# Seven of 21 down products per chunk in three rounded passes instead of one fp32 product

## The reference

```python
scores = sigmoid(x @ gate_weight.T)            # 32 experts, 4 groups, top 2 groups, top 6 experts
g, u = x @ w_gate[e], x @ w_up[e]              # 128 -> 64 for every expert e
eo = (silu(g) * u) @ w_down[e]                 # 64 -> 128
routed = sum_e cw[:, e] * eo[e]
shared = (silu(x @ shared_w_gate) * (x @ shared_w_up)) @ shared_w_down
anchor = one of 16 small experts (128 -> 32 -> 128), by the best expert
out = routed + shared + 0.1 * anchor
```

## Time and profile before

| | |
|---|---|
| median of 3 runs (range) | 1450.74 us (1450.39 to 1451.39) |
| profiled execution, its span | 1452.6 us, 1450.8 us |
| TensorE busy | 1412.9 us (97%) |
| VectorE busy | 1111.2 us (77%) |
| ScalarE busy | 800.2 us (55%) |
| GpSimd busy | 287.6 us (20%) |
| mean granted TensorE clock | 0.995 of full speed |

### The profile page before, as it was taken

The page is one execution under the profiler, slowest core; times in us unless marked ns, Lnnn a source line. Parts: engine busy times, 40 slices in busy tenths (PEclk is TensorE's granted clock), DMA queues, the critical chain, the costliest instruction groups (busy, mean ns, idle before and its releaser), DMA issues.

```text
span 1450.8 us, 27512 instructions
## 1 busy us (share of the span) xinstructions
PE 1412.9 (97%) x9680; PEld 967.3 (67%) x9680; DVE 1111.2 (77%) x2521; ACT 800.2 (55%) x1909; POOL 287.6 (20%) x586
## 2 busy tenths in 40 slices
PE   5999999999989999999999999999899999999998
PEld 4666666666657667676766676676566666666665
DVE  8888888887677777777777777778767877787775
ACT  4344344433457777777777877777544233423422
POOL 1000000000124434444443444344400000000000
PEclk9999999999999999999999999999999999999999
DMA  6432323332300000000000000000033333333332
GB/s 231 162 132 105 112 97 124 107 117 97 116 30 2 2 2 2 2 2 1 2 2 2 2 2 2 1 2 2 2 120 104 126 109 121 110 119 116 119 112 87
DMA packets 59025, 98.07 MB, mean 68 GB/s; under 512 B 6160, under 2 KB 15504, under 8 KB 58896
## 3 DMA queue, kind: packets, MB, share of 16 engines
q1 hardware_dynamic: 58896, 96.38, 19.6%
HBM read 92.68 MB, written 3.67 MB: 66 GB/s over the span
## 4 chain that ended last, share of the span: by engine, by line
PE 86%; DVE 8%; ACT 3%; issue 2%; POOL 0%; DMA 0%; SPq 0%; POOLq 0%; DVEq 0%; ACTq 0%
PE banks L424 19%; PE banks L199 14%; PE banks L201 13%; PE banks L200 13%; PE banks L560 10%; PE banks L525 7%; PE banks L546 5%; PE banks L383 2%; PE banks L535 2%; DVE nmax L1297 2%; ACT work L859 1%; PE banks L395 1%; DVE q_lo L1286 1%; DVE ctx_lo L1317 1%; DVE stage L1312 1%
## 5 line engine op out<-in xcount | busy, mean ns | idle before, releaser
L803 ACT ACTIVATE work<-banks 128x512 f32<-128x512 f32 x320 | 190.9, 597 | 444.5 <-PE banks L201 435.2
L424 PE MATMUL banks<-work,wd 128*128 128x512 f32 x672 | 342.8, 593 | 0.6 <-DVE work L1179 0.4
L1205 DVE TENSOR_TENSOR work<-banks,work 128x512 f32<-128x512 f32 x320 | 220.7, 690 | 147.8 <-ACT work L803 143.4
L859 ACT ACTIVATE work<-banks,nmax 128x512 f32<-128x512 f32 (+3 forms) x512 | 264.4, 528 | 51.9 <-DVE nmax L1297 47.7
L1454 POOL TENSOR_SCALAR work<-work,rrec 128x512 f32<-128x512 f32 (+3 forms) x512 | 261.7, 533 | 0.0
L199 PE MATMUL banks<-xT_hi,wg_hi 128*128 128x512 f32 x336 | 248.0, 738 | 0.5 <-DVE wu_lo L1170 0.4
L1179 DVE TENSOR_TENSOR work<-work 128x512 f32<-128x512 f32 x320 | 226.7, 709 | 5.6 <-DMA work<-cw_rows 1.5
L1297 DVE TENSOR_REDUCE nmax<-banks 128x2 f32<-128x1024 f32 (+3 forms) x256 | 195.6, 806 | 3.1 <-PE banks L535 3.1
L1312 DVE COPY stage<-banks 128x1024 f32<-128x1024 f32 (+1 forms) x128 | 121.9, 952 | 57.9 <-PE banks L546 57.7
L424 PEld LDWEIGHTS banks<-work,wd 128*128 128x128 f32 x672 | 126.2, 189 | 35.3 <-DVE work L1179 4.1
L201 PE MATMUL banks<-xT_hi,wg_lo 128*128 128x512 f32 x336 | 133.4, 397 | 0.0
(11 more groups left out here) (140 smaller groups left out, 2189.6 us busy)
## 6 DMA issues: line engine op xcount, KB each, us to landing
work<-cw_rows SPq DMA_DIRECT2D x320, 256.0 KB, 3.0
x<-in_x SPq DMA_DIRECT2D x8, 256.0 KB, 6.4
out_rows<-x SPq DMA_DIRECT2D x8, 256.0 KB, 2.2
cw_rows<-cwT SPq DMA_DIRECT2D x16, 96.0 KB, 1.9
stage<-in_w_gate SPq DMA_DIRECT2D x3, 448.0 KB, 4.9
wd<-in_w_down SPq DMA_DIRECT2D x3, 448.0 KB, 7.6
stage<-in_w_up SPq DMA_DIRECT2D x2, 448.0 KB, 6.4
stage<-in_wq SPq DMA_DIRECT2D x1, 512.0 KB, 3.8
```

The costliest lines, as they stand in the source:

```text
L424: pe.matmul(psY, wd[:, j * P:(j + 1) * P], z[part_slot(j)], start=j == 0, stop=j == HT - 1, skip_group_check=True).then_inc(s["down_ps"], 1)
L803: nc.scalar.activation(silu[j % 2], psG[j % 3], ACT.Silu) \
L859: m = nc.scalar.activation(prob[:, p % 2, i, o:o + w], ps[:, i, so:so + w], ACT.Exp, bias=nmax[:, p % 2, i, qb:qb + 1], accum_out=rsum[:, ...
L1205: tt(gated[j % 3], psU[j % 3], silu[j % 2], ALU.mult) \
```

## The change

Tiles 0 to 4, 18 and 19 (`SPLIT_Z`) of every chunk, but for tiles 0 to 4 of chunk 0, get their down product by `mm3`, as the gate and up products do. For that:

- the down weights of these seven tiles are put first in memory (`DOWN_ORDER`), loaded into the unused third of `stage` and split once into `wd_parts` (ScalarE in slot 10 of chunk 0, then GpSimd);
- one slot after z is written, ScalarE copies it rounded into `z_parts[0]` (`z_high`, after its silu), and VectorE subtracts this from z into `z_parts[1]` (`z_low`, after its `scale`). For chunk 0 both remainders come at the chunk's end. `z_parts` are the attention's q and k buffers, four slots, idle in the FFN;
- `down` waits for the remainder (`z_lo`) in place of z;
- the input statistics move from slots 3 and 4 to 6 and 9, the square root from 8 to 12;
- to make room in SBUF, `cw` has 48 columns in place of 128 (the rest was zeros), and `sc` and `chosen` lie in `stage`, `wts` in `masked`.

```diff
+SPLIT_Z = [0, 1, 2, 3, 4, 18, 19]
+DOWN_ORDER = SPLIT_Z + [j for j in range(HT) if j not in SPLIT_Z]
...
+        wd_parts = [sb(f"wd_{n}", [P, GT * P], F32R) for n in ("hi", "lo")]
...
-        cw = sb("cw", [P, TB, P])
+        cw = sb("cw", [P, TB, ROWS])
...
+        z_parts = [[t[:, i, :] for t in qk[n] for i in (0, 1)] for n in (0, 1)]
...
+        def splits(g, j):
+            return g * len(SPLIT_Z) - 5 + SPLIT_Z.index(j) + 1
+        def split_z(g, j):
+            return j in SPLIT_Z and not (g == 0 and j < 5)
...
             def down(g, j, first):
-                pe.wait_ge(s["z_done"], tiles(g, j))
+                c = down_columns(j)
                 if j == 0 and not first:
                     pe.wait_ge(s["y_evac"], g)
...
+                if split_z(g, j):
+                    pe.wait_ge(s["z_lo"], splits(g, j))
+                    if g == 0:
+                        pe.wait_ge(wd_split, 1)
+                    mm3(pe, psY, [w[:, c] for w in wd_parts], [t[splits(g, j) % 4] for t in z_parts],
+                        j == 0, False).then_inc(s["down_ps"], 1)
+                    return
+                pe.wait_ge(s["z_done"], tiles(g, j))
...
+            def z_high(g, j):
+                act.wait_ge(s["z_done"], tiles(g, j))
+                nc.scalar.activation(z_parts[0][splits(g, j) % 4], z[part_slot(j)], ACT.Copy) \
+                    .then_inc(s["z_hi"], 1)
...
-                    if 0 < g < NC - 2 and j == 8:
+                    if 0 < g < NC - 2 and j == 12:
                         row_std(g + 2)
...
+                    if setup and j == 20:
+                        z_high(0, 18)
+                    elif not setup and split_z(g, j - 1):
+                        z_high(g, j - 1)
+                if setup:
+                    z_high(0, 19)
                 if first:
                     row_std(2 if setup else STD_FFN)
...
+            def z_low(g, j):
+                dve.wait_ge(s["z_hi"], splits(g, j))
+                tt(z_parts[1][splits(g, j) % 4], z[part_slot(j)], f32(z_parts[0][splits(g, j) % 4]),
+                   ALU.subtract).then_inc(s["z_lo"], 1)
...
-                at_input_stats = 18 if setup else 3
+                at_input_stats, at_input_mean = (18, 19) if setup else (6, 9)
...
                         scale(g, k, first)
+                    if not setup and split_z(g, j - 1):
+                        z_low(g, j - 1)
                 if setup:
                     scale(g, HT - 1, first)
+                    z_low(0, 18)
+                    z_low(0, 19)
```

More of the change, by code:

```diff
@@ L99, in build @@
         wu = [sb(f"wu_{n}", [P, HC - P], F32R) for n in ("hi", "lo")]
-        wd = sb("wd", [P, HC])
+        wd = sb("wd", [P, HC - GT * P])
+        wd_parts = [sb(f"wd_{n}", [P, GT * P], F32R) for n in ("hi", "lo")]
         stage = sb("stage", [P, 2, 3, GT * P])
@@ L134, in build @@
         score = sb("score", [P, TB, E])
-        sc = sb("sc", [P, TB, E])
+        sc, chosen = [stage_flat[:, 4 * PW + i * TB * E:4 * PW + (i + 1) * TB * E]
+                      .rearrange("p (t e) -> p t e", t=TB) for i in (0, 1)]
         t4 = [sb(f"t4_{i}", [P, TB * G, 4]) for i in range(2)]
@@ L147, in build @@
         onehot = sb("onehot", [P, TB, E, TOPK])
-        chosen = sb("chosen", [P, TB, E])
-        wts = sb("wts", [P, TB, E])
+        wts = masked
         wsum = sb("wsum", [P, TB, 1])
@@ L187, in build @@
         spread_loads = [sem(f"s_spread{k}") for k in range(NSPREAD)]
+        wd_split_hi, wd_split = sem("s_wd_split_hi"), sem("s_wd_split")
         wsplit_hi = [sem(f"s_wsplit_hi{k}") for k in range(W_GROUPS)]
@@ L228, in part_slot_free, with down_columns @@
             return tiles(g, j) - (HT if j == HT - 1 else 4 if j > 3 else 5)
+        def splits(g, j):
+            return g * len(SPLIT_Z) - 5 + SPLIT_Z.index(j) + 1
+        def split_z(g, j):
+            return j in SPLIT_Z and not (g == 0 and j < 5)
+        def down_columns(j):
+            o = DOWN_ORDER.index(j) % GT if j in SPLIT_Z else DOWN_ORDER.index(j) - GT
+            return slice(o * P, (o + 1) * P)
         ROUTE = 37
@@ L305, in load_down @@
                 cols = slice(k * GT * P, (k + 1) * GT * P)
-                sp.dma_start(wd[:, cols], wd_in[:, cols]).then_inc(wd_loads[k], 16)
+                dst = stage[:, 0, 2, :] if k == 0 else wd[:, (k - 1) * GT * P:k * GT * P]
+                sp.dma_start(dst, wd_in[:, cols]).then_inc(wd_loads[k], 16)
             def load_x(sp, c):
@@ L363, in _ @@
                 sp.wait_ge(wsplit[k], 2)
+            sp.wait_ge(wd_split, 1)
+            sp.wait_ge(s["down_ps"], 5)
             for w, src in enumerate((wq_in, wk_in)):
@@ L403, in prep_cwT @@
                 pe.wait_ge(s["route"], (g + 1) * ROUTE)
-                to_columns(ps, cw).then_inc(s["cwT_ps"], 1)
+                to_columns(ps[0:ROWS, :], cw).then_inc(s["cwT_ps"], 1)
             def gate_up(g, j, first):
@@ L418, in down @@
             def down(g, j, first):
-                pe.wait_ge(s["z_done"], tiles(g, j))
+                c = down_columns(j)
                 if j == 0 and not first:
                     pe.wait_ge(s["y_evac"], g)
-                if first and g == 0 and j % GT == 0:
-                    pe.wait_ge(wd_loads[j // GT], 16)
-                pe.matmul(psY, wd[:, j * P:(j + 1) * P], z[part_slot(j)], start=j == 0,
+                if split_z(g, j):
[6 more added lines that the diff above has]
+                pe.wait_ge(s["z_done"], tiles(g, j))
+                if first and g == 0:
+                    pe.wait_ge(wd_loads[DOWN_ORDER.index(j) // GT], 16)
+                pe.matmul(psY, (stage[:, 0, 2, c] if j in SPLIT_Z else wd[:, c]), z[part_slot(j)], start=j == 0,
                           stop=j == HT - 1, skip_group_check=True).then_inc(s["down_ps"], 1)
@@ L809, in ffn_chunk @@
                         y_copy(g - 1)
+                    if setup and j == 10:
+                        act.wait_ge(wd_loads[0], 16)
+                        nc.scalar.activation(wd_parts[0][:, :], stage[:, 0, 2, :], ACT.Copy) \
+                            .then_inc(wd_split_hi, 1)
+                    if setup and j == 20:
[4 more added lines that the diff above has]
+                    z_high(0, 19)
                 if first:
@@ L1227, in ffn_chunk @@
                         rows_stats(g + 2)
-                    if g < NC - 2 and j == at_input_stats + 1:
+                    if g < NC - 2 and j == at_input_mean:
                         rows_mean(g + 2, input_stats(g + 2))
@@ L1405, in attention @@
                 dve.wait_ge(s["out_added"], NC)
-            nc.vector.memset(cw[:, :, ROWS:], 0.0)
             nc.vector.memset(z[part_slot(HT - 1)][0:MI, :], 0.0)
@@ L1438, in _ @@
                 split_lo(2, w)
+            pool.wait_ge(wd_split_hi, 1)
+            nc.gpsimd.tensor_tensor(wd_parts[1][:, :], stage[:, 0, 2, :], f32(wd_parts[0][:, :]),
+                                    ALU.subtract).then_inc(wd_split, 1)
             pool.wait_ge(s["small_loaded"], 16)
@@ L1493 @@
         "w_up": hidden_columns(L0_ffn_w_up, L0_ffn_anchor_w_up, []),
-        "w_down": down.reshape(HT, P, D).transpose(1, 0, 2).reshape(P, HT * D),
+        "w_down": down.reshape(HT, P, D)[DOWN_ORDER].transpose(1, 0, 2).reshape(P, HT * D),
         "gate_weight": np.asarray(L0_ffn_gate_weight).T,
```

## The result

| | before | after |
|---|---|---|
| median (range) | 1450.56 us (1448.86 to 1451.52 without one run of 1747.21, 15 runs) | 1447.35 us (1445.99 to 1448.38, 15 runs) |
| ratio | | 0.9979, 95% interval 0.9972 to 0.9986 |
| profiled execution, its span | 1452.6, 1450.8 us | 1447.77, 1446.0 us |
| TensorE, VectorE busy | 1412.9, 1111.2 us | 1400.4, 1170.8 us |

The change gains 3.2 us where 10.0 were forecast, and 1447.35 lies just outside the range of 1433 to 1447. The one run of 1747.21 us stands apart from the other fourteen and leaves the median as it is. The two profiled executions differ by 4.8 us: that of before was 2.0 above its median, that of after 0.4.

A forecast was written before the change was run, and what follows sets the result against it. TensorE's stream was taken to bound the FFN. Terms -17.7 - 1.0 + 2.0 + 3.4 + 0.3 + 1.5 + 1.5 = -10.0 us, from the median of 1450.74 to 1440.7 us; range 1433 to 1447.

The forecast's parts named there:

- Three passes for one product: TensorE's down products: 107 go from 0.863 to 0.697 us, 0.166 less each, 17.7 us in all.
- VectorE's remainders: VectorE: seven subtractions per chunk cost 4.2 us, hidden on average, about 2.9 of its 8.3 us left.
- Boundaries 0/1 and 1/2 to 6/7: Chunk changes in the first FFN: late remainders delay TensorE, costing 2.0, then 3.4 over five, then 0.3 us.
- The second FFN has no statistics in slots 19 and 20 ...: nothing: Second FFN's chunk boundaries: remainder 19 is more than a microsecond early there, so no cost.
- Tolerates some 3 us: Slots 1 to 5: TensorE tolerates some 3 us of VectorE's lag, which shrinks by 0.16 a slot.
- End of the first FFN: TensorE's projection waits behind two more VectorE remainders, 1.2 us, with 0.33 of savings lost: 1.5 us.
- the difference carries over: Whole program: the median stays 1.9 us below the profiled execution, as before, giving 1440.7 us.
- Rival B: All 14 boundaries and slots 0 to 5: ScalarE copies wait for late z; gain only 3.7, 1447 us; chance 0.08.
- A: Boundaries cost nothing because VectorE's small operations overlap more: 1430 to 1432 us; chance 0.12.
- D: TensorE's extra weight loads stand exposed, 0.19 us more per product: slower, 1462 us; chance 0.02.
- E: Three passes between fp32 products cost as much as one of these, so nothing is gained: 1458 us; chance 0.03.
- C: VectorE becomes the bound of the FFN, a chunk lasting 49.7 instead of 49.0 us: slower, 1464; chance 0.04.

The follow-up runs named there:

- passes alone: The changed kernel without the rounded copies of z and the remainders, the three passes reading whatever stands in the buffers: 1434.48 us, ratio 0.9885 against the kernel before.

## Why the prediction was wrong

The mechanism held (rounded passes gain at an even rate, late remainders take back at a few places), the size was not right. By its steps, each with the savings lost in it, in the two profiled executions:

- *Three passes for one product*, -17.7: 0.157 each instead of 0.166, 16.8. The pass interval was taken among fp32 products; among passes alone it is 0.2333. Off by 0.9.
- *VectorE's remainders*, hidden on average: right; the mean load nowhere made TensorE wait.
- *Boundaries 0/1 and 1/2 to 6/7*, 2.0 + 3.4 + 0.3: measured 2.05, five times 0.75, and 0.44. Off by 0.5.
- *"The second FFN has no statistics in slots 19 and 20 ...: nothing"*: **this is the step that failed.** It holds for boundaries 9/10 to 14/15 and not for the first chunk, which I never looked at. Chunk 8 lost 1.4 at slots 4 and 5 and 1.0 at its boundary, 2.4 us in all. "Tolerates some 3 us" was applied without asking how late VectorE is when attention hands over, and the 3 was too much by itself.
- *The weights' split*: "inside the lag that TensorE tolerates: nothing". It was 0.43; other steps in chunk 0 give 0.15 back.
- *The transposes of cw*, -1.0: nothing. Here the bound of nothing was right.
- *End of the first FFN*, 1.5: 2.4. The two remainders stand ahead as forecast, but the projection waits for down product 19, at half clock. No term had the clock. In attention 1.2 come back (last section), which is luck.
- *End of the program*, 1.5: 1.8.

Together 0.9 + 0.5 + 2.4 + 0.4 - 0.15 + 1.0 + 0.9 - 1.2 + 0.3 are 5.1 of the 5.2 between -10.0 and the profiled difference of -4.8. The last 1.6, down to the 3.2 of the medians, is the assumption that "the difference carries over": it was 2.0 for before and 0.4 for after. The clock goes with it. In the 16 executions of the kernel before that were timed beside the experiments, those with a mean granted clock of 0.995 took 1451.0 to 1452.8 us, and of the five with 0.998 four took 1449.8 to 1450.1 and one 1451.6. The profiled execution of before had 0.995. Of the 15 executions of after, 14 had 0.995 and the fastest 0.996.

Rival B named 1447, but not for its reason: it wanted waits at every boundary and in slots 0 to 5, and boundaries 9/10 to 14/15 have none. A falls, since the boundaries cost what they do. D and E fall with passes alone, and C with the chunks 10 to 14, which have all remainders and still gain 1.07 each. Of my own marks of failure none was reached (slots of 2.10 us against 2.12; waits on the new subtraction 7.6 us against 8). The latter are two groups of TensorE's waits (us in total, times, longest):

```profile
PE banks L204 <- DVE k_lo L1232: 4.3, 6, 1.9
...
PE banks L204 <- DVE k_hi L1232: 3.3, 6, 1.5
```

They looked at the passes and at one kind of wait, while a part of the loss was in waits for xn, in the restart of TensorE and in its clock.

## What to carry to other kernels

A cost that is hidden in a steady chunk is to be priced again in each chunk that differs: the first and the last of every stage, and the one that takes over from another stage. List these before summing, and for each ask how late the feeding engine is there. Then use the cheaper form only where it is free: the same seven tiles, with the costly places left in fp32, gain 13 us in place of 3.

## What else the runs showed

TensorE's granted clock fell to half in short stretches in every profile. Where the first FFN ends (busy by engine, clock and DMA as before, in the trace after):

```profile
412.00:418.00 6.00, 4.25 (x10) 2.96 (x11) 3.47 (x6) 1.51 (x4) 0.00 (x0) 0.63 0.00 0
418.00:424.00 6.00, 6.00 (x34) 3.59 (x33) 3.61 (x5) 3.94 (x7) 0.00 (x0) 0.80 0.00 0
```

and in the kernel with 18 and 19 split only where they are free:

```profile
412.00:418.00 6.00, 5.36 (x35) 3.08 (x33) 4.00 (x5) 4.71 (x10) 0.00 (x0) 1.00 0.00 0
```

In the change the clock falls at 413.6, half a microsecond after the wait of 1.90 us, and is back at 420.4: TensorE runs at 1.2 GHz for 6.8 us, through the wait of 0.72 and down product 19.

The five kernels that wait for the remainders of tiles 18 and 19 of chunk 7 (the change and four experiments) all have such a stretch that begins within 6 us of chunk 7's last gate pass. The other five, the kernel before among them, have none there. From the end of the first FFN to the start of the second, the five spend 10 to 14 us at half clock, counted from 3 us windows, passes alone 6.8, and the three that leave these tiles whole 3.4. That stretch of the program lasts 639.7 to 641.8 us in the five, 638.0 with passes alone and 636.4 to 636.9 in the last three. So a wait at the end of a stage came with more than its length.

But the kernel before has 10.2 us at half clock too, from 438 and from 1042 us on. The first stretch has waits of no more than 0.7 us ahead of it; the second begins inside a wait of 2.15 for GpSimd:

```profile
1043.54 1.11 PE L546 MATMUL banks<-small,work 64*128 64x64 f32 x16 [2.15 <-POOL work L1454]
```

Its stretch between the FFNs lasts 639.1 us, against 636.9 in the kernel without tiles 18 and 19. Neither has late remainders there, so the 2.2 us go with 10.2 against 3.4 us at half clock. This is also where the -1.16 of the table comes from. The change falls back by 1.2 us more up to 420.6, at half clock; before loses 1.5 at 438, and near the end of attention, where before has 6.8 us at half clock and after 3.4, another 0.8. Which waits bring the clock down was not tested, and one profile of each kernel does not settle it.
